# Replacing the first norm of a two-norm layer, from the second block on, by centred cos and sin matrices and a damped second eps

## The reference

```python
def layernorm(x):  # over the last axis
    return (x - mean(x)) / sqrt(var(x) + 1e-5)

def rfs(xw):       # ab = xis, AB = exp(xis)
    dots = xw @ (ab[:, None] * proj_matrix).T
    return 1 / sqrt(512) * AB * exp(dots - 0.5 * sum(xw * xw) * ab * ab)

x = layernorm(x + rfs(x) @ rfs(input_weights).T)
real = x @ cos(theta + theta_noise)
imag = x @ sin(phi + phi_noise)
x = layernorm(x + sqrt(real * real + imag * imag))
```

## Time and profile before

| | us |
|---|---|
| time, median of 3 runs | 727.46 (727.32 to 727.57) |
| time of the profiled execution | 727.33 |
| its span | 725.5 |
| TensorE (PE) busy | 708.5 (98%) |
| VectorE (DVE) busy | 563.8 (78%) |
| ScalarE (ACT) busy | 489.7 (68%) |
| GpSimd (POOL) busy | 279.2 (38%) |

### The profile page before, as it was taken

How to read it: one execution, slowest core, us unless ns; L and a number is a source line. 1 busy time by engine, 2 the same in 40 slices (tenths; PEclk the granted TensorE clock), 3 DMA queues, 4 the chain that set the end, 5 groups by cost and what they waited for, 6 DMA issues and landing times.

```text
span 725.5 us, 10937 instructions
## 1 busy us (share of the span) xinstructions
PE 708.5 (98%) x3228; PEld 582.8 (80%) x3228; DVE 563.8 (78%) x963; ACT 489.7 (68%) x760; POOL 279.2 (38%) x465
## 2 busy tenths in 40 slices
PE   8999999999999999999999999999999999999993
PEld 7876788888888888888888888888888888888872
DVE  5799789797777868778786877869687777877686
ACT  7746757584957769395775939677594867757463
POOL 5765026606144250614416062341605235160525
PEclk9999999999999999999999999999999999999998
DMA  8761032310403232050322205032130503200011
GB/s 301 221 136 54 15 115 69 122 59 27 162 15 118 70 106 67 15 173 15 116 72 81 92 15 173 15 116 72 61 113 15 171 17 116 70 32 29 1 58 58
DMA packets 32753, 60.80 MB, mean 84 GB/s; under 512 B 3168, under 2 KB 3168, under 8 KB 32736
## 3 DMA queue, kind: packets, MB, share of 16 engines
q1 hardware_dynamic: 31584, 58.50, 24.3%
q0 software_dynamic: 1152, 2.10, 1.7%
HBM read 43.78 MB, written 16.81 MB: 84 GB/s over the span
## 4 chain that ended last, share of the span: by engine, by line
PE 90%; DVE 5%; ACT 2%; POOL 1%; issue 1%; POOLq 0%; ACTq 0%; DVEq 0%
PE token_ps L910 9%; PE token_ps L912 9%; PE token_ps L911 9%; PE token_ps L815 8%; PE token_ps L813 8%; PE token_ps L814 7%; PE project_ps L763 7%; PE project_ps L761 7%; PE project_ps L762 7%; PE turn_ps L824 4%; PE project_ps L910 3%; PE project_ps L912 3%; PE project_ps L911 3%; PE token_ps L843 1%; PE token_ps L841 1%; PE token_ps L842 1%
## 5 line engine op out<-in xcount | busy, mean ns | idle before, releaser
L398 POOL TENSOR_TENSOR late<-late 128x1024 f32<-128x1024 f32 x29 | 71.6, 2470 | 306.7 <-ACT late L671 306.7
L761 PE MATMUL project_ps<-xT_hi,gs_hi 128*128 128x512 f32 x248 | 100.1, 404 | 0.0
L813 PE MATMUL token_ps<-W_hi,F_hi 128*128 128x512 f32 x256 | 99.7, 389 | 0.0
L815 PE MATMUL token_ps<-W_hi,F_lo 128*128 128x512 f32 x256 | 99.6, 389 | 0.0
L814 PE MATMUL token_ps<-W_lo,F_hi 128*128 128x512 f32 x256 | 99.6, 389 | 0.0
L763 PE MATMUL project_ps<-xT_hi,gs_lo 128*128 128x512 f32 x248 | 97.1, 392 | 0.0
L762 PE MATMUL project_ps<-xT_lo,gs_hi 128*128 128x512 f32 x248 | 96.7, 390 | 0.0
L586 ACT ACTIVATE late<-late 128x1024 f32<-128x1024 f32 x29 | 30.8, 1062 | 77.1 <-POOL late L398 77.1
L671 ACT ACTIVATE late<-late 128x1024 f32<-128x1024 f32 x54 | 57.2, 1059 | 33.1 <-DVE late L1400 28.8
L646 ACT ACTIVATE z<-z,shift,rstd 128x512 f32<-128x512 f32 x56 | 45.2, 808 | 40.0 <-POOL shift L393 40.0
L1138 DVE TENSOR_TENSOR z<-token_ps,x_tok 128x512 f32<-128x512 f32 x64 | 44.1, 689 | 30.9 <-PE token_ps L815 27.6
(11 more groups left out here) (214 smaller groups left out, 1802.7 us busy)
## 6 DMA issues: line engine op xcount, KB each, us to landing
x_tok<-in_x SPq DMA_DIRECT2D x16, 1024.0 KB, 5.6
out_tokens<-o_tile SPq DMA_DIRECT2D x62, 256.0 KB, 2.2
plain_xT_lo<-in_xT SPq DMA_DIRECT2D x14, 1024.0 KB, 5.3
norm_bc<-token_norms SPq DMA_DIRECT2D x15, 256.0 KB, 3.0
plain_T_hi<-in_gsT SPq DMA_DIRECT2D x4, 256.0 KB, 4.3
z<-in_wT SPq DMA_DIRECT2D x4, 256.0 KB, 4.6
plain_T_lo<-in_xT SPq DMA_DIRECT2D x1, 1024.0 KB, 7.9
plain_T_hi<-in_theta SPq DMA_DIRECT2D x4, 256.0 KB, 6.5
```

Of the source, the lines that this page charges most:

```text
L398: pool.tensor_tensor(parts[:, p, :, 0, :], parts[:, p, :, 0, :], parts[:, p, :, 1, :], ALU.add).then_inc(sum_made, 2)
L761: nc.tensor.matmul(o, gs_hi[:, c, cols], rhs_hi[:, c, :], start=(c == 0), stop=False)
L813: nc.tensor.matmul(o, F_hi[:, c, cols], W_hi[:, c, :], start=(c == 0), stop=False)
L815: return nc.tensor.matmul(o, F_lo[:, c, cols], W_hi[:, c, :], start=False, stop=(c == C - 1))
```

## The change

From block 1 on no first norm is applied. z keeps the residual sum y; turns wait for `y_made`. After block 0's sines, GpSimd sums the four chunks of cos and of sin (`sum_chunks`), TensorE sums these over partitions with ones, after mix j=0 and j=1 of block 1, ScalarE copies the result over 512 as the columns' means (`copy_mean`), GpSimd subtracts them in place from the whole cos and sin (`centre`), ScalarE rounds and VectorE splits the centred matrices anew. GpSimd's `make_damp` computes eps times (v + eps) for the four tiles of a block, and the second norm's inverse root adds that instead of eps. Statistics of y are still made, since v is needed. Block 0 keeps its first norm. The second residual adds z, now y, to the magnitude of y's products.

```diff
+        chunk_sums = [late[:, 0:2], late[:, 2:4]]
+        column_means = [late[:, 1, :], late[:, 3, :]]
...
-            def scale1(b, j):
-
-                root1(b, j)
-                pool.tensor_tensor(neg_mean[:, j:j + 1], mv[:, j, 0:1], minus_one[:, 0:1], ALU.mult).then_inc(neg_mean_made, 1)
...
-                pool.tensor_tensor(shift[:, j:j + 1], neg_mean[:, j:j + 1], rstd[:, j:j + 1], ALU.mult).then_inc(shift_made, 1)
...
+            def make_damp(b):
+                pool.wait_ge(mv_made, C * (b + 1))
+                pool.tensor_tensor(damp[:, :], mv[:, :, 1], eps[:, :], ALU.add).then_inc(damp_made, 1)
+                pool.wait_ge(damp_made, 2 * b - 1)
+                pool.tensor_tensor(damp[:, :], damp[:, :], eps[:, :], ALU.mult).then_inc(damp_made, 1)
+
+            def sum_chunks(k, raw):
+
+                pool.wait_ge(sine_made, 4 * C)
+                pool.tensor_tensor(chunk_sums[k], raw[:, 0:H, :], raw[:, H:C, :], ALU.add).then_inc(chunk_sums_made, 1)
+                pool.wait_ge(chunk_sums_made, 2 * k + 1)
+                pool.tensor_tensor(chunk_sums[k][:, 0, :], chunk_sums[k][:, 0, :], chunk_sums[k][:, 1, :],
+                                   ALU.add).then_inc(chunk_sums_made, 1)
+
+            def centre(k, raw, parts_made):
+                pool.wait_ge(parts_made, C)
+                pool.wait_ge(mean_copied, k + 1)
+                for c in range(C):
+                    pool.tensor_tensor(raw[:, c, :], raw[:, c, :], column_means[k], ALU.subtract).then_inc(centred, 1)
...
+                pool.wait_ge(damp_made, 2 * b)
+                pool.tensor_tensor(var_eps2[:, both], mv2[:, both, 1], damp[:, both], ALU.add).then_inc(var2_made, 2)
...
+            sum_chunks(0, theta_turns)
+            sum_chunks(1, phi_turns)
+
+            centre(0, theta_turns, cos_made)
+            centre(1, phi_turns, sin_made)
             for j in range(C):
-                root1(1, j)
-            for j in range(C):
-                root2(0, j)
+                root2(0, j, eps[:, 0:1])
+            make_damp(1)
             pair_sum(1, 0)
             pair_residual2(1, 0)
 
             def step(b):
                 pair_sum(b - 1, 1)
-                scale1(b, 0)
                 pair_scale2(b - 1, 0)
-                scale1(b, 1)
                 pair_scale2(b - 1, 1)
-                scale1(b, 2)
-                scale1(b, 3)
+                make_damp(b)
...
+                copy_mean(0)
+                copy_mean(1)
+                round_centred(0, cos_hi[:, 0:H, :], theta_turns[:, 0:H, :])
+                round_centred(1, cos_hi[:, H:C, :], theta_turns[:, H:C, :])
+                round_turned(0)
+                features(C * (b + 2), 0, 0)
+                round_centred(2, zT_hi[:, :, 4 * Q:6 * Q], phi_turns[:, 0:H, :])
+                round_turned(1)
+                features(C * (b + 2) + 1, 1, 1)
+                round_centred(3, low_sin_hi[:, :, :], phi_turns[:, H:C, :])
+                for j in range(2, C):
+                    round_turned(j)
                     features(C * (b + 2) + j, j, j % 2)
...
-                def norm1(j):
-                    act.wait_ge(shift_made, C * s + j + 1)
-                    nc.scalar.activation(z[:, j, :], z[:, j, :], ACT.Identity, scale=rstd[:, j:j + 1],
-                                         bias=shift[:, j:j + 1]).then_inc(z_made, 1)
...
             def turn(b, j):
-                pe.wait_ge(z_made, C * b + j + 1)
+                pe.wait_ge(y_made, C * b + j + 1)
...
                     mix(b, j)
+                    if j < 2:
+
+                        pe.wait_ge(chunk_sums_made, 2 * (j + 1))
+                        nc.tensor.matmul(turn_ps[j][:, :], ones[:, :], chunk_sums[j][:, 0, :],
+                                         start=True, stop=True).then_inc(mean_done, 1)
...
+                    if j < 2:
+                        pe.wait_ge(mean_copied, j + 1)
                     plain_turn(b, j)
                 for j, part in PHASE_ORDER:
                     use = 2 * j + part
+                    pe.wait_ge(centred_lo_made, H * (part + 1))
...
+                def split_centred(n, lo, raw, hi):
+
+                    dve.wait_ge(centred_hi_made, n + 1)
+                    lower(lo, raw, hi).then_inc(centred_lo_made, 1)
...
+                split_centred(0, cos_lo[:, 0:H, :], theta_turns[:, 0:H, :], cos_hi[:, 0:H, :])
                 split_turned(b, 0)
                 next_exponent(b, slot, 1)
-                plain_norm1(b, 3)
+                split_centred(1, cos_lo[:, H:C, :], theta_turns[:, H:C, :], cos_hi[:, H:C, :])
                 split_features(C * (b + 2), 0)
                 split_turned(b, 1)
                 next_exponent(b, slot, 2)
+                split_centred(2, zT_lo[:, :, 4 * Q:6 * Q], phi_turns[:, 0:H, :], zT_hi[:, :, 4 * Q:6 * Q])
                 split_features(C * (b + 2) + 1, 1)
                 split_turned(b, 2)
                 next_exponent(b, slot, 3)
+                split_centred(3, low_sin_lo[:, :, :], phi_turns[:, H:C, :], low_sin_hi[:, :, :])
```

More of the change, by code:

```diff
@@ L451, in _ @@
             pair_scale2(NB - 1, 0)
-            root2(NB - 1, 2)
-            root2(NB - 1, 3)
+            root2(NB - 1, 2, damp[:, 2:3])
+            root2(NB - 1, 3, damp[:, 3:4])
         @block.scalar
@@ L596, in second_step, with copy_mean, round_centred, round_turned @@
                 b = 1
-                for j in range(C):
+                def copy_mean(k):
+                    act.wait_ge(mean_done, k + 1)
+                    nc.scalar.activation(column_means[k], turn_ps[k][:, :], ACT.Copy, scale=1.0 / D).then_inc(mean_copied, 1)
+                def round_centred(n, hi, raw):
+                    act.wait_ge(centred, H * (n + 1))
+                    nc.scalar.activation(hi, raw, ACT.Copy).then_inc(centred_hi_made, 1)
+                def round_turned(j):
                     act.wait_ge(turn_done, C * b + j + 1)
                     nc.scalar.activation(turned(zT_hi, j), turn_ps[j % 2][:, :], ACT.Copy).then_inc(zT_hi_made, 1)
+                copy_mean(0)
[10 more added lines that the diff above has]
+                    round_turned(j)
                     features(C * (b + 2) + j, j, j % 2)
```

40 lines of the change are left out of this document (15 added, 25 removed).

## The result

The changed kernel took 729.56 us in the median of 8 runs (728.47 to 730.67), beside 727.57 for the kernel before on the same chip (727.32 to 728.85): a ratio of 1.0023, 95% interval 1.0012 to 1.0034. It is slower by a quarter of a per cent, and the interval, which starts at 1.0012, doesn't reach 1. The profiled execution of the changed kernel took 729.21 us with a span of 727.2, so 2.01 lie around the span, where the kernel before had 1.83.

The account below looks back on a forecast made before the run. TensorE was taken to bound the kernel, never waiting in the loop. From 727.33 us, 1.75 for two products, 0.35 and 0.30 for meetings, and 0 for loop and last block gave 729.7 us, range 728.7 to 731.6.

Parts of the forecast that it names:

- The two fp32 products: Block 1, after mix j=0 and j=1: two products with ones on TensorE, 0.87 us each, add 1.75 us unhidden.
- The meetings: Before 81 us: GpSimd's chunk sums and VectorE's F_lo splits exclude each other, delaying TensorE by 0.65 us; bounds 0 and 1.7.
- The first term (0.35): First block: F_lo waits for GpSimd's first sum until 73.9, so exponent j=2 and L841 come 0.35 us late.
- The second term (0.30): The fourth F_lo split ends near 81.2, so block 1's mix j=0 starts 0.3 us later still.
- The loop at nothing: Loop: TensorE never waits, so removing norms gains 0 and the pitch stays 42.7 us.
- The last block at nothing: Last block: turn j=3 starts 0.59 us sooner, but M6 still waits for the half-sum split; gain taken 0.
- two small later breaks at 0.26: Last block: later breaks in the products' pitch, at most 0.26 us of possible gain, an estimate, beside the 0.59 bound.
- that rival: Not slower, last block pays back: half-sum split ends before 697.9, gaining 0.85; 728.2 us without meetings; chance 0.11.
- Centring late: Rival, 88 to 101 us: VectorE meets GpSimd's subtractions and phases wait up to 2.2 us; 731.9, likelier near 731; chance 0.10.
- the terms as predicted (2.40): Whole kernel: 1.75 for two products, 0.35 and 0.30 for meetings, 0 for loop and last block.
- Only the products count: Rival, before 81 us: GpSimd's sums fall between VectorE's operations, so only 1.75 us is added: 729.1 us; chance 0.12.

Follow-up runs that it names:

- the two repeats: The changed kernel run again without edit, beside the kernel before: 729.28 us (ratio 1.0024), and on a third chip 729.53 us (ratio 1.0023).
- The run that forces this order: Changed kernel, with GpSimd's first sum waiting until VectorE's last sine split in the first block is done: 730.01 us, ratio 1.0031.
- the run with late sums: Changed kernel, with GpSimd's chunk sums waiting until VectorE's eighth F_lo split of the first block is done: 735.24 us, ratio 1.0103.
- moving two lines and adding a wait: Kernel before, with the last block's output norms of tiles 2 and 3 behind the second pair's roundings: 727.32 us (ratio 0.9995), again 727.53 us (0.9993).

## Why the prediction was right, and where it was not

The forecast of 729.7 us stands 0.14 over the first median and 0.2 to 0.4 over the two repeats, but its terms were less right than their sum. As a difference it was farther off: 2.4 over the kernel before, where the three pairs of medians differ by 1.46 to 1.99.

*The two fp32 products: right, a little small.* 1.75 was predicted, 1.88 measured in the trace, 1.85 with them taken out. The row-to-row price of 0.87 held exactly; what the earlier trace rows couldn't show is the 0.06 ahead of each, between the last fp32r product and the fp32 one.

*The meetings: the mechanism was right, the size four times too large.* 0.65 was predicted, 0.16 measured. The first term (0.35) took the order split, then sum. The run that forces this order shows 0.37. In fact the sum is issued while the split runs and ends 0.21 sooner. The second term (0.30) needed the fourth F_lo to end at 81.2; it ended at 80.74, 0.13 ahead of the mix product. It was hidden by hardly more than nothing, and the run with late sums shows what stands behind that cover.

*The loop at nothing: right.* The pitch is 42.7, and putting 41.9 us back into ScalarE changed no start in it.

*The last block at nothing: wrong by 0.48.* The argument was right for M6, which follows the half-sum split to the hundredth (it starts 2.22 later with 2.20 at the block's first mix product). The bound named two small later breaks at 0.26 as a possible gain and took none of it. Both breaks were there, and larger: by the starts in the trace of before, the two steps around M4 (705.29 to 705.99) and around M2 (706.91 to 707.56) take 0.70 and 0.65 us instead of 0.45 each, 0.44 more in all. The 0.26 came from idle time, and modelled ends that overlap the next start hide a part of a break. The step that failed is to have followed the removed norm only to the next product. Its queue went on: two output norms and the second pair's roundings stood behind it, then VectorE's splits and joins, and two products waited for the banks that these free. The gain has another size than that rival's too: it hung on a half-sum split before 697.9, and that didn't come.

*Centring late: it didn't happen.* VectorE's last split of sin stands at 107.39 for 1.21 us and phase (0,1) starts at 109.14, with no wait on it. The prediction had 108.1 and 109.2.

*What was missed.* The fall of the clock, traced once in the changed kernel and likely in two of its 27 runs, was in no term and no rival; the traced execution of before showed 1.00 up to its last product. It is a small part of the median and marks two of the five runs over 730.3. Against the terms as predicted (2.40), the trace has 1.56 (1.88 + 0.16 - 0.48), and 0.32 of start scatter, small rest and time around the span, which another execution could have had the other way. So the sum was close partly by luck: *Only the products count*, at 729.1, describes the stages ahead of the last block better: 2.04 measured beside its 1.75, where the forecast had 2.40.

## What to carry to other kernels

Take work from an engine only after asking which wait of the bounding engine it ends: 45 us of ScalarE's and 51 of GpSimd's were worth 0.48 us, all of it in the last block, and two products on TensorE took four times as much. Of a removed instruction, follow its whole queue and not only its next reader; the gain that was here shows in the traces just as well after moving two lines and adding a wait. And before putting GpSimd work into its idle time, look at which VectorE operations with two SBUF inputs lie beside it: a meeting can hold VectorE for up to the length of one GpSimd operation, so the place matters more than the sum (between 0.16 and 5.8 us for the same four additions).

## What the runs showed of the hardware

*A meeting of VectorE and GpSimd has a price that can be read ahead.* VectorE's operation with two SBUF inputs of 512 columns ended 0.55 us behind the end of the GpSimd operation it met, in five places of three kernels, and several of them in a row got one turn between two GpSimd operations. The Trainium skill (SBUF — State Buffer, Who interferes with whom) says that whoever issues first holds the shared port pair for the whole instruction and the other blocks; the 7.25 us for three operations of 0.6 agree with it, and add that the two engines then take turns. One meeting alone holds only for what is left of the other's operation: 0.16 us for the first F_lo.

*TensorE's clock fell behind an idle time of 1.8 us in some executions and not in others.* Three traces have it, behind 1.81, 2.09 and 2.74 us of idle time: it fell from 2.4 to 1.2 GHz 1.1 to 1.5 us after work had begun again and came back some 3 us later, at a cost of 1.66 us in the first. Six other traces with 1.81 to 1.84 us, and one with 2.02, kept 1.00. By the mean clock of a run, which is only a sign, it came in 1 of 75 runs of the kernel before (1.67), 2 of 27 of the changed one (1.81) and 4 of 6 behind 2.09 and 0.48.

*An fp32 product of 512 columns costs 0.94 us among fp32r products of 0.227*, 0.87 from its start and 0.06 ahead of it, and two fp32r products in its place 0.47.
